# Wo as three float32r products, with its units and the tail's first down product at other steps

## The reference

```python
q, k, v = (jnp.einsum('bsd,hde->bhse', x, W) for W in (Wq, Wk, Wv))
scores = jnp.where(causal, q @ k^T / sqrt(64), -inf)
out = softmax(scores) @ v
y = layernorm(x + heads @ Wo, eps=1e-3) * gamma + beta     # heads: B, S, 1024
x = layernorm(x + y)
x = layernorm(x + (silu(x @ wg^T) * (x @ wu^T)) @ wd^T)
```

## Time and profile before

| | us |
|---|---|
| median of 3 runs | 1460.8 |
| lowest and highest | 1460.03, 1463.27 |
| the profiled execution | 1462.12 |
| its span, from the first to the last instruction | 1459.7 |
| PE busy in the span | 1403.6 (96%) |
| DVE, ACT, POOL busy | 1014.0, 1003.8, 1003.9 (69% each) |

### The profile page before, as it was taken

How to read it: one execution, slowest core, us unless ns; L and a number is a source line. 1 busy time by engine, 2 the same in 40 slices (tenths; PEclk the granted TensorE clock), 3 DMA queues, 4 the chain that set the end, 5 groups by cost and what they waited for, 6 DMA issues and landing times.

```text
span 1459.7 us, 23745 instructions
## 1 busy us (share of the span) xinstructions
PE 1403.6 (96%) x7936; PEld 1227.6 (84%) x7936; DVE 1014.0 (69%) x2729; ACT 1003.8 (69%) x1924; POOL 1003.9 (69%) x944
## 2 busy tenths in 40 slices
PE   6999999999999999999999999999999999999876
PEld 5788888888888888888888888888888888888766
DVE  7766666766666676776667676776766667677874
ACT  4776777767676676766668676686867668676534
POOL 4676766666686775868668586785868668587744
PEclk9999999999999999999999999999999999999988
DMA  4333222312342221321232122132223223122000
GB/s 135 97 81 96 64 60 95 116 52 68 108 131 72 61 88 53 90 85 44 88 116 95 52 59 68 59 117 55 78 66 102 88 59 95 52 59 59 23 11 30
DMA packets 61241, 110.45 MB, mean 76 GB/s; under 512 B 16256, under 2 KB 41600, under 8 KB 61120
## 3 DMA queue, kind: packets, MB, share of 16 engines
q1 hardware_dynamic: 61120, 108.94, 25.0%
HBM read 60.95 MB, written 13.89 MB: 51 GB/s over the span
## 4 chain that ended last, share of the span: by engine, by line
PE 81%; DVE 9%; POOL 4%; ACT 3%; issue 2%; DMA 1%; ACTq 0%; SPq 0%; POOLq 0%
PE bank L787 24%; PE bank L760 16%; PE bank L660 12%; PE bank L736 9%; PE bank L723 7%; PE bank L685 5%; PE bank L822 5%; PE bank L834 3%; POOL probs_lo L1403 2%; DVE K L1121 1%; DVE max_part L1156 1%; POOL h_lo L1445 1%; DVE bank L1154 1%; ACT probs_hi L972 1%; ACT probs L969 1%
## 5 line engine op out<-in xcount | busy, mean ns | idle before, releaser
L1403 POOL TENSOR_TENSOR probs_lo<-probs,probs_hi 128x512 fp32r<-128x512 f32 x576 | 744.1, 1299 | 401.0 <-ACT probs_hi L972 397.8
L969 ACT ACTIVATE probs<-bank 128x512 f32<-128x512 f32 x576 | 344.4, 598 | 304.4 <-DVE bank L1170 219.5
L760 PE MATMUL bank<-Q,K 128*128 128x512 f32 (+3 forms) x1536 | 385.3, 352 | 5.2 <-ACT probs_hi L972 4.5
L972 ACT ACTIVATE probs_hi<-bank 128x512 fp32r<-128x512 f32 x576 | 342.6, 595 | 0.0
L760 PEld LDWEIGHTS bank<-Q,K 128*128 128x128 f32 x1536 | 252.8, 190 | 33.6 <-ACT probs_hi L972 5.7
L736 PE MATMUL bank<-K,Q 128*128 128x512 f32 (+3 forms) x768 | 245.6, 362 | 8.4 <-DVE max_part L1154 6.3
L1154 DVE CUSTOM_DVE_ANT_0 bank<-bank,mask_keys_free 128x128 f32<-128x128 f32 (+3 forms) x512 | 243.3, 506 | 3.4 <-PE bank L736 3.0
L787 PE MATMUL bank<-probs_hi,VH 128*128 128x512 f32 (+3 forms) x768 | 232.0, 343 | 6.0 <-POOL probs_lo L1403 5.3
L787 PE MATMUL bank<-probs_lo,VH 128*128 128x512 f32 (+3 forms) x768 | 234.6, 346 | 0.0
L787 PE MATMUL bank<-probs_hi,VL 128*128 128x512 f32 (+3 forms) x768 | 234.4, 346 | 0.0
L1170 DVE TENSOR_TENSOR bank<-bank,mask_queries_free 128x256 f32<-128x256 f32 (+1 forms) x320 | 119.6, 374 | 148.1 <-PE bank L760 147.0
(11 more groups left out here) (170 smaller groups left out, 2224.3 us busy)
## 6 DMA issues: line engine op xcount, KB each, us to landing
Q<-Q SPq DMA_DIRECT2D x64, 256.0 KB, 3.7
K<-K SPq DMA_DIRECT2D x64, 256.0 KB, 3.4
recip_bc<-recip_scratch SPq DMA_DIRECT2D x62, 256.0 KB, 3.4
wh<-w_scratch SPq DMA_DIRECT2D x12, 768.0 KB, 4.9
wl<-w_scratch SPq DMA_DIRECT2D x12, 768.0 KB, 6.6
wo_quad<-wo SPq DMA_DIRECT2D x16, 256.0 KB, 3.2
y<-x SPq DMA_DIRECT2D x16, 256.0 KB, 3.4
x_tail<-x SPq DMA_DIRECT2D x13, 256.0 KB, 3.1
```

What stands on the lines that cost most here:

```text
L760: last = mm(bk[:, at:at + cols], KX[:, n, P * i:P * i + P], QX[:, n, q0:q0 + cols], start=(KX is K1 and at == 0), stop=(KX is K2 and at + ...
L969: A(pe_[:, g % 2, :], stb[g % 2][:, :], ACT.Exp).then_inc(exp_done, 1)
L972: A(ph[:, g % RING, :], stb[g % 2][:, :], ACT.Exp).then_inc(hi_done, 1)
L1403: G.tensor_tensor(pl[:, g % RING, :], pe_[:, g % 2, :], ph[:, g % RING, :].bitcast(F32), ALU.subtract).then_inc(lo_done, 1)
```

## The change

- Wo and the heads are each split into high and low parts, and a Wo unit becomes twelve float32r products of 256 columns in place of four float32 ones (iterations 0 to 14; the Wo product of the last iteration stays as it was).
- ACT copies Wo to `wo_hi` in step 28 (`wo_split`), DVE subtracts to get `wo_lo` (`wo_rest`). One step ahead of each Wo unit ACT copies the 256 columns of two `heads_T` slots to `h_hi` (`heads_split`) and DVE makes `h_lo` (`heads_rest`). These two tiles are the tail's own; for the last group of units, pieces of `xl` are used.
- The Wo units move from steps 12, 14, 15, 21 to 14, 16, 18, 21. Their banks change from 1, 1, 0, 1 to 1, 0, 1, 1. The tail's first `t_down` moves from step 13 to step 12.
- Wo is loaded at step 17, not 23. `row_sums` goes away to make room: the sums' row is put into `recip_bc`, and the last steps use the mask tile.

```diff
-WO_AT, WO_AT_LAST = [12, 14, 15, 21], [11, 13, 15, 16]
+WO_AT, WO_AT_LAST = [14, 16, 18, 21], [11, 13, 15, 16]
+WO_LOAD_AT, WO_SPLIT_AT = 17, 28
-STEADY = tail_at(-5, -1, 7, [9, 23, 29], [13, 26, 32], 36)
+STEADY = tail_at(-5, -1, 7, [9, 23, 29], [12, 26, 32], 36)
...
+            def wo_split(it):
+                act.wait_ge(wo_loaded, 16 * (it + 1))
+                act.wait_ge(wo_mm, 4 * it)
+                A(WoH[:, :, :], WoS[:, :, :], ACT.Copy).then_inc(wo_hi, 1)
+
+            def heads_split(wi, u):
+                if u % 2 == 0:
+                    act.wait_ge(ht_norm, 4 * wi + 3 + u // 2)
...
+                elif u == 0 and running(wi + 1):
+                    act.wait_ge(tpe[0], NPE * (wi + 1 - TAIL_LAG) + PEC["d0"])
+                else:
+                    act.wait_ge(wo_mm, 4 * wi + u)
+                A(heads_parts(wi, u)[0], heads_rows(wi, u), ACT.Copy).then_inc(heads_hi, 1)
...
+            def wo_rest(it):
+                dve.wait_ge(wo_hi, it + 1)
+                V.tensor_tensor(WoL[:, :, :], WoS[:, :, :], WoH[:, :, :].bitcast(F32), ALU.subtract).then_inc(wo_lo, 1)
+
+            def heads_rest(wi, u):
+                dve.wait_ge(heads_hi, 4 * wi + u + 1)
+                hi, lo = heads_parts(wi, u)
+                V.tensor_tensor(lo, heads_rows(wi, u), hi.bitcast(F32), ALU.subtract).then_inc(heads_lo, 1)
...
+                            for n, (X, W) in enumerate(((hi, WoH), (lo, WoH), (hi, WoL))):
+                                last = mm(bk[:, D * t:D * t + D], X[:, a, P * t:P * t + P], W[:, r, :],
+                                          start=(r == 0 and n == 0), stop=(r == 1 and n == 2))
...
                 else:
-                    pe.wait_ge(proj_lo, 2 * proj_unit(it + 1, 0, 2) + 2)
+                    pe.wait_ge(proj_lo, 2 * proj_unit(it + 1, 0, 2 * u - 4) + 2)
...
+                    if c == 0:
                         act.wait_ge(sums_loaded, 16 * h)
+                        act.wait_ge(ht_norm, 2 * pair)
-                    A(rsum[0:1, cols], pvb[c][0:1, :], ACT.Copy).then_inc(ht_copied, 1)
+                    A(RB[E:E + 1, cols], pvb[c][0:1, :], ACT.Copy).then_inc(ht_copied, 1)
```

More of the change, by code:

```diff
@@ L570, in step @@
                     f_load(FINAL_LOAD_AT.index(s))
+                if s == WO_LOAD_AT and live:
+                    load_wo(it)
                 if s == 18 and 0 <= it < NQ - 1:
@@ L637, in proj @@
             def proj(it, pair, u):
-                if u >= 2:
+                if u == 2 and pair == 0 and it >= 2:
+                    pe.wait_ge(y_added, 4 * (it - 2) + 3)
+                elif u >= 2:
                     pe.wait_ge(proj_lo, 2 * proj_unit(it, pair, u - 2) + 2)
@@ L722, in wo_unit @@
                     for r in range(2):
[L723 to L724 removed]
+                        if it == NIT:
+                            last = mm(bk[:, D * t:D * t + D], HT[:, (2 * wi + r) % 3, tok:tok + P], WoS[:, r, :],
+                                      start=(r == 0), stop=(r == 1))
+                        else:
+                            a = heads_at(wi, r)
+                            for n, (X, W) in enumerate(((hi, WoH), (lo, WoH), (hi, WoL))):
+                                last = mm(bk[:, D * t:D * t + D], X[:, a, P * t:P * t + P], W[:, r, :],
+                                          start=(r == 0 and n == 0), stop=(r == 1 and n == 2))
                 last.then_inc(wo_mm, 1)
@@ L986, in last_copy @@
                     A(HT[own, slot, cols], pvb[n - HA][own, :], ACT.Copy)
-                    A(rsum[own, cols], pvb[n - HA][other, :], ACT.Copy).then_inc(ht_copied, 1)
+                    A(maskS[own, :], pvb[n - HA][other, :], ACT.Copy).then_inc(ht_copied, 1)
             def copy_out(h, c):
@@ L1070, in step @@
                         v_evac(v_due(g - 1, u), u)
+                for u in range(4):
+                    if wo_due(g + 1, u) is not None:
+                        heads_split(wo_due(g + 1, u), u)
                 if 0 <= g < NG:
                     exp(g)
+                if s == WO_SPLIT_AT and 0 <= it < NIT - 1:
+                    wo_split(it)
                 if has_pieces(it) and s in RAW_HI_AT:
@@ L1338, in step @@
                         v_rest(v_due(g - 1, u), u)
+                for u in range(4):
+                    if wo_due(g + 1, u) is not None:
+                        heads_rest(wo_due(g + 1, u), u)
+                if s == WO_SPLIT_AT and 0 <= it < NIT - 1:
+                    wo_rest(it)
                 h, k = divmod(g - (C1_DONE + LAG + 2), NS)
```

58 lines of the change are left out of this document (36 added, 22 removed).

## The result

| | before | after |
|---|---|---|
| median, us | 1461.9 (4 runs on the same chip) | 1486.97 (4 runs) |
| lowest and highest | 1460.03, 1463.27 | 1486.08, 1487.87 |
| ratio, 95% interval | | 1.0172, 1.0160 to 1.0184 |
| profiled execution, its span | 1462.12, 1459.7 | 1486.60, 1484.8 |

The change makes the kernel 1.7% slower. The prediction had the sign and the place; the size was forecast at 0.9%, and the time lies 1 us above the upper end of its range. The granted clock was 0.990 against 0.991, so the clock has no part in it.

A forecast was written before the change was run, and what follows sets the result against it. PE, 96% busy, was taken as the bound. A gain of 18.0 us and waits of 3.3, 3.1, 11.9, 6.7, 2.5, 1.8 and 1.5 summed to +12.8 us: 1473.6 us, 0.9% slower, range 1466 to 1481 us.

The forecast's parts named there:

- the unit gains 18.0: All 60 Wo units of iterations 0 to 14: each gains 0.29 to 0.30 us on PE, -18.0 us in all.
- The estimate by four passes: Wo units: true FP32 takes four passes, so the gain is 28.6 us; as a rival 1463.0 us, chance 0.03.
- PE busy near 1385 us: Sign for the changed kernel's profile: PE busy near 1385 us in a longer span.
- Step 12: First down product, moved to step 12, waits 0.33 us for h's low part in iterations 5 to 14: +3.3 us.
- step 18: Wo unit at step 18 waits 0.22 us for Q's low parts to free its bank, 14 times: +3.1 us.
- the smaller term for iterations 1 to 4: `raw_piece` and `heads_rest(0)` on DVE ahead of step 14's mask, with POOL's backlog: 0.45 us in each iteration, +1.8 us.
- Step 21: Unit at step 21 waits 0.85 us for `heads_rest` of step 20, behind POOL's `probs_lo`, 14 times: +11.9 us.
- Low part of Wo: `wo_rest` in step 28 waits for POOL and delays step 29's mask: +6.7 us in iterations 0 to 4, +2.5 steady.
- Costs at nothing: Sixty-odd other ACT copies, Wo's load at step 17 and the odd heads' wait for `norm`: no cost; ACT idles 31%.
- rival of a second collision: Step 15: `heads_rest(1)` also waits for POOL, delaying step 16's unit: 9.8 us more, 1483 us; chance 0.12.
- DVE wins at step 20: Rival: at step 20 DVE starts before POOL, so step 21's unit waits for nothing: 1461.7 us, no change; chance 0.13.
- The waits are hidden: Rival: DVE seldom waits for POOL and the rests run in 0.6 us: 1452.0 us, faster; chance 0.17.

## Why the prediction was right in sign and half the size

**PE bounds, and the unit gains 18.0: right.** From the kernel with the moved units to the one without the rests, steps 14 to 22 are 1.17 to 1.20 us shorter in each of iterations 1 to 14, and iteration 15 is 0.85 shorter: 17.5 us, 0.29 a unit. Less the 3.0 of the row of sums that is 14.5, and the time falls by 14.9. The estimate by four passes, 28.6, is ruled out. One sign that the prediction gave was wrong all the same: PE busy near 1385 us. It was 1405.7, since the busy rows cover part of the waits. And a reading was incomplete: in the steady iterations 5 to 15 PE waits longest not for POOL but for DVE's maximum, 0.52 us in step 6, while most of the 5.3 us for `probs_lo` fall in step 12 of iterations 1 to 4. No term of the sum used it.

**Step 12, step 18: the waits right, their cost too small.** Forecast 0.33 and 0.22, measured 0.32 and 0.23 by the rows. The term was sized as the wait; what PE loses is the wait and 0.10 us for the slow first product. That is 2.4 us over both places. About 0.1 more in each iteration is spread over steps 14, 17 and 19. Of the smaller term for iterations 1 to 4 (1.8 forecast) the moved units alone bring 0.8, in steps 12 and 13 of iterations 3 and 4. The moves cost 10.1 us by the times and 10.7 by the steps, and not 8.2.

**Step 21: mechanism right to the hundredth, size 15.1 in place of 11.9.** The exponential of step 20 was placed 1.99 to 2.09 us behind the step's start (it came at 2.09), DVE's low part of K ends 3.29 behind (3.29 by the earlier trace rows too), and the lead of POOL was put at 0.07 to 0.17 (0.06). The wait was worked out from the middle of the span for POOL and a hand-over of 0.05; it came at its late end, the hand-over from DVE took 0.15 (757.39 to 757.54), and the first product was slow by 0.07. 0.85 became 1.08. The upper bound of 0.95 had left out the restart.

**Low part of Wo: 6.7 + 2.5 forecast, 7.2 + 1.5 measured.** The 0.55 that DVE needs after POOL's end was exact.

**"Costs at nothing": this step failed.** It covered "sixty-odd ACT copies" by ACT's idle share of the whole span. The copies are nearly free: the kernel without the rests still has them, and by its steps it differs from the one with the moved units by the products, by step 3 and by 0.5 us in steps 12 and 13 of iteration 3; what else differs (steps 8 and 26 of single iterations, the time up to step 4 of iteration 0) differs between the other kernels too, with either sign. But the row of sums, which stays one copy of the same length, was not costed at all, and it costs 3.0 to 3.5 us, because ACT has next to no slack between steps 34 and 3. The share of idle time is an average, and these steps had no part in it.

**Steps 15 and 16, 2.0 us: the "smaller" term, its mechanism right and its place not.** The prediction had `raw_piece` with `heads_rest(0)` on DVE ahead of the mask of step 14, at 0.45 in iterations 1 to 4. It costs 0.33 to 0.45, but in the five iterations that have both a rest and a raw piece there: 1, 2, 3, 7 and 11, not 4. Step 14 of iteration 7, first the changed kernel, then the one without the rests (POOL is ahead of the raw piece's low part in the first and behind it in the second):

```profile
646.03 0.69 DVE L1258 TENSOR_TENSOR h_lo<-heads_T,h_hi 128x512 fp32r<-128x512 f32 x1
646.42 1.44 POOL L1477 TENSOR_TENSOR probs_lo<-probs,probs_hi 128x512 fp32r<-128x512 f32 x1 [0.25 <-ACT probs_hi L1003]
646.80 1.61 DVE L1199 TENSOR_TENSOR xl<-raw,xh 128x512 fp32r<-128x512 f32 x1
648.34 0.42 DVE L1230 TENSOR_TENSOR bank<-bank,mask_queries_free 128x256 f32<-128x256 f32 x1
```

```profile
628.75 0.62 DVE L1199 TENSOR_TENSOR xl<-raw,xh 128x512 fp32r<-128x512 f32 x1
629.30 0.41 DVE L1230 TENSOR_TENSOR bank<-bank,mask_queries_free 128x256 f32<-128x256 f32 x1
```

The rest makes the raw piece's low part second. It takes 1.61 rather than 0.62, and the mask behind it starts 2.46 behind the step's start (645.88) rather than 0.86 (628.44). The step absorbs most of that, and a third of a microsecond or a little more reaches steps 15 and 16. That this delay is what reaches PE there is argued from the rows; no run took it away alone. The rival of a second collision is another matter and didn't come: PE waits for a rest only ahead of the unit of step 21 and once in iteration 15. In most iterations the rest of step 15 comes first and POOL is stretched, where PE has slack for it (iteration 8: the rest from 739.20 for 0.68, POOL from 739.47 for 1.57).

**The sum.** The difference of 12.3 us between the forecast +12.8 and the spans' +25.1 is: step 21 3.2, row of sums 3.0, steps 15 and 16 2.0, the moves 1.9 to 2.5 (their restarts, less the 1.0 of the smaller term that they don't bring), iteration 15 0.9, the start before the first scores 1.0 (which varies by as much from one execution to the next), less 0.5 for Wo; 0.2 to 0.8 is left over. All errors but one have one sign. The steps that failed are two: the rest ahead of step 21 was the right wait, sized 3.2 us too small, and the row of sums was a cost put at nothing without a look at its steps. Each term was read as the wait of one engine at one place; none had the small costs around a wait, and operations "at nothing" had no price. The range's upper end was built from the same terms.

**The rivals.** "DVE wins at step 20" didn't come, by 0.06 us, and the run with the useless copy shows that this case was real: 0.08 us decide over 15 us. "The waits are hidden" fell: in the changed kernel every rest that starts while POOL has more than 0.2 us to go waits, and those of 512 columns end 0.55 us after POOL.

## What to carry to other kernels

- When two engines that share a path to SBUF start within a tenth of a microsecond of each other, look at which one is on the critical path and make it first, if need be by delaying the other. One instruction of 0.19 us was worth 15 us here.
- Cost a new wait of PE as the wait and a restart of about 0.1 us on top, and read it from the distances of starts, not from the busy rows.
- Before an operation is called free, look at its engine's gaps in the very steps where it stands. A wait that is taken away pays only if the loop behind it is not as tight: check the next step's start.

## What the runs showed of the hardware

- **ACT overlaps an instruction with the one before by 0.10 us, but only on the same first partition.** Distances: 0.50 behind a copy of 0.59 that stays on partition 0, 0.61 where the next one starts on another (64 to 0, 0 to 64, 32 to 0), 0.28 behind one of 0.38 with both on 64. In the changed kernel the second of each pair of Q and of K copies, on partition 64, starts 0.02 behind the end of the first, 128 times of 128; of the pairs of VH copies, both on partition 0, all 64 overlap by 0.10. What counts seems to be the last instruction that used the same memory, and not only the one just ahead: in step 20 the exponential (from PSUM) stands behind the heads' copy (from SBUF to SBUF), both on partition 0, and is held all the same in all 14 iterations (754.39 against 753.74 + 0.63), where the last to read PSUM was K's second copy, on partition 64. Where it follows the same copy at once in steps 13, 15 and 17, it overlaps by 0.09 or more. No run tests this alone. The Trainium skill (VectorE: DVE Perf Modes, Two Vector instructions with no wait between them) states such a rule as a model for VectorE: an instruction is held until all earlier ones have ended when an input starts in another group of 32 partitions than the last read of that memory did, or its output in another than the last write. These rows show the like on ScalarE.
- **PE's first product of 256 columns after a wait is followed by the second after 0.19 to 0.22 us, not 0.12.** Seen in steps 12, 18 and 21. One of 512 columns, in step 3: 0.33, not 0.23.
- **DVE and POOL, both reading SBUF:** DVE 0.69 alone and 1.77 when second by 0.06 us; POOL 1.29 alone, 1.82 when second by 0.02 us, and 1.57 when second by 0.27 us. Whoever is second ends 0.55 (DVE, with the other ahead by 0.06 to 0.86) or 1.15 (POOL, by 0.02 to 0.5) after the first.
